# Two turns change places in the attention loop: the third block of probabilities and the queries of the next unit

## The reference, cut to what matters

```python
ln_out = _ln(_layernorm(x), ln_w, ln_b)
q, k, v = fp8_linear(ln_out, wq), fp8_linear(ln_out, wk), fp8_linear(ln_out, wv)   # q and k: _ln over D
core = softmax(q @ k.T / sqrt(D)) @ v
qx, kx, vx = fp8_linear(ln_out, wqx), cond @ wkx.T, cond @ wvx.T                   # qx and kx: _ln over D
xout = softmax(qx @ kx.T / sqrt(D)) @ vx
catq = div_clamp_fp8(concat(core, xout), proj_smooth)                              # rounded to FP8
x = x + tanh(g_xattn) * (catq @ wproj.T) * scales
x = x + tanh(g_ffn) * moe(_layernorm(x))
```

## Time and profile before

| what | value |
|---|---|
| median of 3 runs | 820.9 us (820.71 to 822.23) |
| profiled execution | 819.82 us, span 818.0 us |
| mean granted TensorE clock | 0.961 |
| PE busy | 726.0 us, 89% |
| DVE busy | 613.4 us, 75% |
| ACT busy | 466.6 us, 57% |
| POOL busy | 459.7 us, 56% |
| chain of waits, by engine | PE 62%, DVE 20%, issue 6%, ACT 5%, POOL 4% |

### The profile page before, as it was taken

The page is one execution under the profiler, slowest core; times in us unless marked ns, Lnnn a source line. Parts: engine busy times, 40 slices in busy tenths (PEclk is TensorE's granted clock), DMA queues, the critical chain, the costliest instruction groups (busy, mean ns, idle before and its releaser), DMA issues.

```text
span 818.0 us, 15329 instructions
## 1 busy us (share of the span) xinstructions
PE 726.0 (89%) x4859; PEld 589.4 (72%) x4859; DVE 613.4 (75%) x1290; ACT 466.6 (57%) x1178; POOL 459.7 (56%) x592
## 2 busy tenths in 40 slices
PE   2548999899999989999998999998886886999996
PEld 2546787778788778878787878887664654777775
DVE  6867888788888878889887898987876592444554
ACT  3656867677676767867667686775652231222221
POOL 3464777566777756777775767776673213222220
PEclk9779999999999999999999999999999596999999
DMA  5320000100010010001001010000020103666661
GB/s 181 97 64 1 27 27 1 52 27 27 1 40 15 1 53 26 26 7 48 1 1 53 1 33 27 1 3 0 1 60 0 64 2 110 191 187 189 199 192 53
DMA packets 44478, 42.74 MB, mean 52 GB/s; under 512 B 3717, under 2 KB 43386, under 8 KB 44410
## 3 DMA queue, kind: packets, MB, share of 16 engines
q1 hardware_dynamic: 42874, 36.62, 14.8%
q0 software_dynamic: 1536, 5.28, 2.4%
HBM read 39.52 MB, written 2.37 MB: 51 GB/s over the span
## 4 chain that ended last, share of the span: by engine, by line
PE 62%; DVE 20%; issue 6%; ACT 5%; POOL 4%; SPq 2%; DMA 1%; POOLq 0%; DVEq 0%; ACTq 0%
PE out_ps L1718 8%; PE proj_ps L1458 7%; PE s_ps L1502 6%; PE proj_ps L1443 5%; PE pT_ps L1511 5%; PE aux_ps L1521 5%; PE aux_ps L1535 5%; DVE q_tok L1086 5%; PE aux_ps L1472 4%; PE proj_ps L1434 4%; PE work_ps L1710 3%; POOL rstd L527 3%; PE work_ps L1732 2%; DVE ss L1066 2%; DVE pT_sb L1111 2%
## 5 line engine op out<-in xcount | busy, mean ns | idle before, releaser
L542 POOL TENSOR_SCALAR p_sb<-p_sb,psum_row 128x256 f32<-128x256 f32 x256 | 125.8, 507 | 69.0 <-DVE psum_row L1105 67.7
L796 ACT ACTIVATE p_sb<-s_ps,negmax 128x256 f32<-128x256 f32 x256 | 118.5, 473 | 66.3 <-DVE negmax L1100 65.2
L1521 PE MATMUL aux_ps<-pT_sb,v_sb 128*128 128x512 f32 x256 | 122.3, 601 | 6.1 <-DVE pT_sb L1111 6.1
L1111 DVE COPY pT_sb<-pT_ps 128x512 f32<-128x512 f32 x128 | 87.7, 686 | 47.5 <-PE pT_ps L1511 46.8
L1502 PE MATMUL s_ps<-kT,qT 128*128 128x256 f32 x768 | 112.7, 289 | 8.2 <-DVE qT L1096 4.6
L549 POOL TENSOR_TENSOR y_bf<-y_bf,mg_bf 128x512 bf16<-128x512 bf16 x64 | 86.0, 1343 | 58.5 <-DVE mg_bf L1123 58.5
L1502 PEld LDWEIGHTS s_ps<-kT,qT 128*128 128x128 f32 x768 | 98.0, 190 | 18.3 <-issue 18.3
L1100 DVE TENSOR_REDUCE negmax<-s_ps 128x2 f32<-128x512 f32 x128 | 86.5, 683 | 5.9 <-PE s_ps L1502 5.6
L527 POOL TENSOR_TENSOR rstd<-var,minus_half 128x8 f32<-128x8 f32 (+1 forms) x64 | 86.6, 1354 | 5.5 <-POOL var L523 0.4
L552 POOL TENSOR_TENSOR catq<-y_bf,mg_bf 128x512 fp32r<-128x512 bf16 x64 | 79.5, 1242 | 5.0
L1535 PE MATMUL aux_ps<-wpT,catq 128*128 128x256 f32 x512 | 71.0, 293 | 7.5 <-DVE wkvT L1017 4.8
(11 more groups left out here) (174 smaller groups left out, 1381.4 us busy)
## 6 DMA issues: line engine op xcount, KB each, us to landing
w_up_a<-in_L_ffn_gate_up_proj SPq DMA_DIRECT2D x16, 384.0 KB, 3.5
w_up_b<-in_L_ffn_gate_up_proj SPq DMA_DIRECT2D x16, 384.0 KB, 3.5
wp_raw<-in_L_xattn_wproj SPq DMA_DIRECT2D x16, 256.0 KB, 2.9
w_down_a<-in_L_ffn_down_proj SPq DMA_DIRECT2D x16, 192.0 KB, 3.5
w_down_b<-in_L_ffn_down_proj SPq DMA_DIRECT2D x16, 192.0 KB, 3.5
w_raw<-in_L_xattn_w_kv_x SPq DMA_DIRECT2D x8, 256.0 KB, 4.0
w_raw<-in_L_xattn_wq SPq DMA_DIRECT2D x7, 256.0 KB, 2.6
w_raw<-in_L_xattn_wqx SPq DMA_DIRECT2D x7, 256.0 KB, 2.9
```

The lines of the kernel that those rows point to most:

```text
L542: ins = nc.gpsimd.tensor_scalar(p_sb[:, r, st, :], p_sb[:, r, st, :], rsum[:, r, st:st + 1], 1.0, ALU.mult, ALU.mult)
L796: ins = nc.scalar.activation(p_sb[:, r, st, :], s_ps[:, r % 2, st, :], ACT.Exp, bias=negmax[:, r, st:st + 1], accum_out=psum_row[:, r, st: ...
L1111: nc.vector.tensor_copy(pT_sb[:, r // 2, r % 2, :, :], pT_ps[:, r % 2, :, :]).then_inc(pT_ready, 1)
L1521: ins = nc.tensor.matmul(aux_ps[:, f.bank, :], v_sb[:, (2 * s.n + tt) % VRING, ty, s.gi, :], pT_sb[:, ty, :, tt, :], start=(tt == 0), stop ...
```

## The change

In TensorE's loop, the turn of block 2 of s1 moves ahead of the turn of the queries of s0. No instruction is added or taken away, no wait is changed, and the other engines' orders stay as they are.

```diff
                 if s1:
                     fill_pv(s1, 0)
+                if s1:
+                    fill_pT(s1, 2)
                 if s0:
                     fill_Tq(s0, 0)
-                if s1:
-                    fill_pT(s1, 2)
                 if s0 and s0.gi == 0:
                     fill_Tk(s0.n, 1)
```

## The result

The changed kernel takes 828.65 us (median of 6 runs, 825.58 to 829.58), the one before 820.81 us (median of 6): the ratio is 1.0095, with a 95% interval of 1.0076 to 1.0114. The forecast was 829.0 us.

A forecast was written before the change was run, and what follows sets the result against it. TensorE, busy 89%, was taken as the bound, paced behind even iterations by VectorE's chain. Terms -2.5 + 0.1 + 8.6 + 0.6 + 1.3 gave +8.1 us, so 829.0 us, range 817.5 to 831.5.

The forecast's parts named there:

- TensorE starts at GpSimd's end + 0.05 us: Turn of probabilities in TensorE's loop: 0.02 us lost where inputs arrive together, 0.23 us gained where the scaling comes later.
- the twelve odd iterations of the second kind: Odd iterations, without 31, whose scaling had waited for GpSimd's rstd: TensorE starts sooner, together -2.5 us.
- The keys' remainder ends 0.80 us later: VectorE in even iterations, behind GpSimd's second rounding step: ten at +0.80 us, iteration 2 at +0.6, together +8.6 us.
- the even iterations without weights: Iterations 4, 8, 12, 16, 20, 24, 28, no weights to turn behind them: scores wait for VectorE's chain, +0.80 us each.
- Iterations 6, 14 and 22: 0.2 us each: Even iterations covered by other weights: 0.6 of the 0.8 us hidden, 0.2 us paid each, together +0.6 us.
- Iterations 30 and 31: +1.3 us: No key projection behind them; next scores wait for the queries' remainder itself: +0.79 and +0.54 us.
- the longest remainder of keys: Line 1096 on VectorE, 3.642 us at the start: counted among the cross-attention remainders that meet the rounding step.
- Rival 1: Keys' remainder goes right behind the queries' one, before the second rounding step: -3.1 us, 817.8 us; chance 0.20.

The follow-up runs named there:

- the kernel with even swaps: Turns change places in even iterations only, against the kernel before: 830.29 us against 819.62, ratio 1.0129.
- the order of before with the added wait: Kernel before, but in even iterations GpSimd's second rounding step waits until VectorE has formed the keys' remainder: 820.59 us, ratio 1.0006.
- the order of before with short rounding steps: Kernel before with GpSimd's two rounding steps cut to 2 of 512 columns from subunit 2 on: 809.95 us, ratio 0.9861.

## Why the prediction was right

By its steps, with the measured steps between the scaling of one iteration and the next in the profile after:

- *TensorE starts at GpSimd's end + 0.05 us.* In iteration 16 it starts 0.08 us behind the scaling, 0.06 before: 0.02 us lost. The steps behind the twelve odd iterations of the second kind are -0.18 to -0.23 us, together -2.5 us, as forecast.
- *The keys' remainder ends 0.80 us later.* 0.79 in the trace above. The steps behind the even iterations without weights are 0.79 to 0.80 us, behind 2, 10, 18 and 26 they are 0.73 to 0.78; for iteration 28, which the clock hides, the kernel with even swaps gives 0.76. Sum of the eleven: 8.6 us, as forecast. The remainder itself took 1.64 to 1.65 us in the 15 iterations, and that of the queries 1.42 to 1.44 us in 30 of 31 (1.63 in iteration 2), as named in advance.
- *Iterations 6, 14 and 22: 0.2 us each.* This term was too small: 0.43 to 0.45 us each, 1.3 us together. I counted only the wait of the scores for the remainder. The copy of the fourth block is late as well, and the product with the values (line 1521), which stands ahead of the covering weights, waits for it: in iteration 15 it starts 6.44 us behind the scaling, 6.06 before. It is the wait that grew from 5 to 15 times.
- *Iterations 30 and 31: +1.3 us.* Too large. Behind iteration 30 the load for the scores starts 0.78 us later (forecast 0.79), but at the next scaling 0.47 us of it are left. Behind 31 it starts 3.92 us behind the scaling, 3.40 before: 0.52 us (forecast 0.54). These are still there at the end of the last rounding step: 30.95 us behind the scaling, and 30.43 in the order of before with the added wait, whose clock fell at the same distance behind it (30.7 us, 30.8 in the kernel after). Together 1.0 us.

The steps add up to -2.5 + 0.1 + 8.6 + 1.3 + 1.0 = 8.5 us, where 8.1 were forecast; between the medians 7.8 were measured, with an interval of 6.2 to 9.4. The two mis-sized terms, one 0.7 us too small and one 0.3 too large, partly cancel, and the median lies below the sum of the steps: that 829.0 came within 0.4 us of 828.65 is in part luck.

One reading in the prediction was wrong and cost nothing: the longest remainder of keys, 3.642 us, did not meet a rounding step. It belongs to the self-attention keys of iteration 0, before there is anything to round, and ran beside another subtraction of GpSimd (line 510, 4.06 us from 58.78).

Rival 1, VectorE keeping the port, did not come about. The second rounding step is recorded from 348.37, 0.39 us ahead of the keys' remainder, so it asked first; no run shows whether 0.06 us would have turned the order. The Trainium skill (SBUF — State Buffer, "A bandwidth-pool intuition that's wrong") gives some 115 ns between VectorE's end and a blocked GpSimd's going on, measured there for the descriptors of a DMA; by that figure the prediction let VectorE's next instruction win, and it did not.

How close the handover lies to the recorded end stays open. Counted back from its end (348.37 + 1.49 = 349.86), the 1.17 us of work of the second rounding step begin at 348.69, 0.14 us *before* the recorded end (348.83) of the remainder that blocked it. From that, as from the earlier trace rows, the prediction took it that the port comes free before the recorded end. In the order of before with short rounding steps, a step on 2 columns ends at 344.09, 0.06 us behind the end of the remainder that held it up (344.03), though it takes 0.20 us by itself:

```profile
343.35 0.68 DVE L1097 TENSOR_TENSOR qT<-qk_f,qT 128x512 fp32r<-128x512 f32 x1
343.52 0.57 POOL L550 TENSOR_TENSOR y_bf<-y_bf,mg_bf 128x2 bf16<-128x2 bf16 x1 [1.36 <-DVE mg_bf L1124]
```

That fits a port that comes free early, and as well a start of the instruction that needs no port and runs while it waits; the sums come out the same, since they use the measured distances.

The rule of the exclusive port, which the Trainium skill gives on the same page ("Who interferes with whom"), agrees with the measurements here: the keys' remainder, 0.68 us by itself, is recorded with 1.65 us where the second rounding step came first, and with 0.68 us where that step was made to wait.

## What to carry to other kernels

A swap on one engine that adds no work can still turn round who is first on two others; follow both moved results to the next pair of instructions that exclude each other, and ask who then waits on the path. Of two that exclude each other, let the one that nobody waits for give way by a wait of its own. Time a step by the stage in which it stands: a saving in the loop and one where the pipeline runs dry were very different in size here.

## What the runs showed of the hardware

- Time spent waiting for the port counts as busy time of the waiting instruction: VectorE's busy time rose by 26.5 us without any more work, and the same subtraction is recorded with 0.68, 1.35, 1.43 or 1.65 us. In the order of after with the rounding steps cut to 2 columns it takes 0.67 to 0.73 us from iteration 3 on.
- A GpSimd instruction that already waits gets in between two VectorE instructions that follow each other at once: in iteration 16 the keys' remainder is recorded from 348.76, with no idle time behind the queries' one, and yet, counted back from its end by 0.68 us, it works only from 349.73, when the second rounding step (to 349.86) is all but through.
- A rounding step on 2 columns takes 0.20 us (in the order of after, the first step, mean 197 ns), on 512 columns 1.16 us.
